# Masks of a sparse attention added by TensorE instead of VectorE, with a new order of the pieces (l2 attention of a twelve-stage decoder)

## The reference

```
ss = einsum('bhsd,bhmd->bhsm', q4, ks4) * SCALE
causal_sel = arange(s)[None, :, None] >= pos[:, None, :]
a_sel = _masked_softmax(ss, (causal_sel & valid[:, None, :])[:, None])
...
wmask = (cols <= rows) & (cols > rows - WIN)
a_win = _masked_softmax(sw, wmask[None, None])
...
g = softmax(x @ Wg + bg, axis=-1)
out = g[..., 0:1] * out_comp + g[..., 1:2] * out_sel + g[..., 2:3] * out_win
return out @ Wo + bo
```

## Time and profile before

| what | value |
|---|---|
| median of three runs | 2348.35 us (2347.89 to 2351.34) |
| the profiled execution, its own time | 2353.02 us |
| its span in the profile | 2351.2 us |
| TensorE busy | 1899.7 us, 81% |
| VectorE busy | 1656.8 us, 70% |
| ScalarE busy | 1021.0 us, 43% |
| GpSimd busy | 605.2 us, 26% |
| granted TensorE clock, mean | 0.843 |

### The profile page before, as it was taken

The page is one execution under the profiler, slowest core; times in us unless marked ns, Lnnn a source line. Parts: engine busy times, 40 slices in busy tenths (PEclk is TensorE's granted clock), DMA queues, the critical chain, the costliest instruction groups (busy, mean ns, idle before and its releaser), DMA issues. The chain is left out here.

```text
span 2351.2 us, 31000 instructions
## 1 busy us (share of the span) xinstructions
PE 1899.7 (81%) x11181; PEld 1074.3 (46%) x11186; DVE 1656.8 (70%) x3766; ACT 1021.0 (43%) x1648; POOL 605.2 (26%) x528
## 2 busy tenths in 40 slices
PE   4788888889788989999997677668885766699983
PEld 2444554536363333577775555545332322334321
DVE  6665848665678878644457988984479988976546
ACT  1226646464743635633332232232354446335562
POOL 0002324242331010000002633520146534631100
PEclk8888999989997777999998778766877877789955
DMA  4001213030402000000000000000000000000000
GB/s 168 1 0 47 58 31 74 10 95 1 103 2 93 1 1 1 23 1 1 1 1 10 1 1 1 1 1 1 0 1 0 0 0 0 0 1 1 1 5 14
DMA packets 19224, 44.32 MB, mean 19 GB/s; under 512 B 5323, under 2 KB 7935, under 8 KB 18047
## 3 DMA queue, kind: packets, MB, share of 16 engines
q1 hardware_dynamic: 19071, 42.33, 6.4%
HBM read 17.15 MB, written 1.05 MB: 8 GB/s over the span
## 5 line engine op out<-in xcount | busy, mean ns | idle before, releaser
L2440 POOL TENSOR_TENSOR l_attn_lane_u<-l_attn_lane_xp,l_attn_lane_bn 128x512 f32<-128x512 f32 x128 | 177.2, 1412 | 192.4 <-ACT l_attn_lane_bn L2411 152.3
L2358 PE MATMUL lane_banks<-l_attn_lane_hc,base 128*128 128x512 f32 x256 | 165.7, 764 | 58.3 <-DVE l_attn_lane_hc L2498 58.2
L2489 DVE TENSOR_TENSOR_SCAN l_attn_lane_h<-l_attn_lane_da,l_attn_lane_u 128x512 f32<-128x512 f32 x128 | 188.5, 1508 | 11.3 <-ACT l_attn_lane_da L2419 8.0
L604 POOL TENSOR_SCALAR lane_next_rstd<-lane_next_mv 128x4 f32<-128x4 f32 x48 | 12.2, 253 | 697.3 <-DVE lane_next_mv L581 697.2
L1728 ACT ACTIVATE l_ffn_lane_hT<-lane_banks,weights 128x512 f32<-128x512 f32 x128 | 87.9, 687 | 145.1 <-PE lane_banks L1682 144.5
L1774 DVE SCALAR_TENSOR_TENSOR l_ffn_lane_eo<-lane_banks,l_ffn_lane_sel,l_ffn_lane_eo 128x128 f32<-128x128 f32 x224 | 63.0, 344 | 101.4 <-PE lane_banks L1704 100.8
L1704 PEld LDWEIGHTS lane_banks<-weights,l_ffn_lane_hT 128*128 128x128 f32 x1024 | 119.8, 192 | 15.9 <-issue 12.2
L1526 ACT ACTIVATE l_attn_lane_ex<-lane_banks 128x512 f32<-128x512 f32 x160 | 84.1, 667 | 98.3 <-PE lane_banks L1440 97.6
L1704 PE MATMUL lane_banks<-weights,l_ffn_lane_hT 128*128 128x128 f32 x1024 | 122.8, 276 | 0.9 <-DVE l_ffn_lane_eo L1774 0.9
L2358 PEld LDWEIGHTS lane_banks<-l_attn_lane_hc,base 128*128 128x128 f32 x256 | 56.6, 238 | 131.9 <-DVE l_attn_lane_hc L2498 87.8
L2037 POOL TENSOR_TENSOR l_attn_lane_qb<-l_attn_lane_qT,base 128x512 f32<-128x512 f32 x64 | 87.8, 1382 | 97.8 <-PE lane_banks L1939 84.3
(11 more groups left out here) (525 smaller groups left out, 4685.5 us busy)
## 6 DMA issues: line engine op xcount, KB each, us to landing
f_attn_lane_vb<-f_attn_lane_work SPq DMA_DIRECT2D x192, 64.0 KB, 2.0
weights<-packed SPq DMA_DIRECT2D x1, 4564.5 KB, 13.4
f_attn_lane_work<-f_attn_lane_work SPq DMA_DIRECT2D x64, 64.0 KB, 2.0
f_attn_lane_vb<-f_attn_lane_va SPq DMA_DIRECT2D x8, 512.0 KB, 4.5
f_attn_lane_vb<-f_attn_lane_va SPq DMA_DIRECT2D x8, 384.0 KB, 5.9
weights<-packed SPq DMA_DIRECT2D x1, 2320.0 KB, 8.6
weights<-packed SPq DMA_DIRECT2D x1, 2091.0 KB, 14.1
weights<-packed SPq DMA_DIRECT2D x1, 1263.0 KB, 5.4
```

The costliest lines, as they stand in the source:

```text
L2358: pe.matmul(ps(2 + c), w("ident"), hc[:, c, :], start=(n == 1), stop=(n == NS)).then_inc(*s.up("state_added"))
L2440: g.tensor_tensor(u[:, i % 3, :], dtx[:, c, :], bn[:, n % 2, :], ALU.mult).then_inc(*s.up("u_ready"))
L2489: v.tensor_tensor_scan(h[:, c, :], da[:, i % 3, :], u[:, i % 3, :], 0.0, ALU.mult, ALU.add).then_inc(*s.up("scanned"))
```

## The change

In `l2_attn`:
- `mask` becomes 16-bit. TensorE puts it into the score bank first, as the 16-bit identity by the mask broadcast to four head groups, and the four score matmuls accumulate on top. `mask_ready` is new and is awaited before the first scores.
- ScalarE copies the finished scores from PSUM to `sc` and signals `masked`; VectorE's addition is gone.
- Tiles are scored eight ahead of the turns instead of five, so two groups are scored before the first is turned. VectorE's order becomes shift 0, shift 1, weigh 0, weigh 1, shift 2, pick 0, weigh 2, shift 3, pick 1, weigh 3, pick 2, pick 3. ScalarE takes the exps of groups 0 and 1 together after tile 7.
- GpSimd spreads ten tiles, multiplies groups 0 and 1, spreads the other six, and multiplies groups 2 and 3.
- The bias is added to x by GpSimd at the unit's start. The values of blocks and selected tokens are copied into `vall` by ScalarE after tile 2.

```diff
-    mask = sb("mask", [P, J, C])
+    mask = sb("mask", [P, J, C], BF16)
...
+        pe.wait_ge(*s.at("mask_ready", 1))
 
         def scores(j):
+
             yield
             if j >= 2:
                 pe.wait_ge(*s.at("masked", j - 1))
             pe.wait_ge(*s.at("qb_ready", j + 1))
+            bank = ps(j % 2)[:, 0:4 * C].rearrange("p (g c) -> p g c", g=4)
+            pe.matmul(bank, net.w16("ident16"), bc(mask[:, j, :], 4), start=True, stop=False)
             for g in range(4):
-                last = pe.matmul(ps(j % 2)[:, g * C:(g + 1) * C], qb[:, j % 2, tile(g)], kall[:, j, :], start=True, stop=True)
+                last = pe.matmul(bank[:, g, :], qb[:, j % 2, tile(g)], kall[:, j, :], start=False, stop=(g == 3))
             last.then_inc(*s.up("scores_in_psum"))
...
-        for i in range(J + 6):
-            if 5 <= i < J + 5:
-                yield from turn(i - 5)
+
+        for i in range(J + 2 * GR + 1):
+            if 2 * GR <= i < J + 2 * GR:
+                yield from turn(i - 2 * GR)
             if i < J:
                 yield from scores(i)
-            if i >= 6:
-                yield from values(i - 6)
+            if i >= 2 * GR + 1:
+                yield from values(i - 2 * GR - 1)
...
-            if i % GR == GR - 1 and i < J:
+            if i < J:
                 g = i // GR
+                yield
+                act.wait_ge(*s.at("scores_in_psum", i + 1))
+                if g >= 2:
+                    act.wait_ge(*s.at("pT_in_psum", i - 2 * GR + 1))
+                act.activation(sc[:, g % 2, i % GR, :, :], ps(i % 2)[:, 0:4 * C].rearrange("p (g c) -> p g c", g=4), ACT.Copy)\
+                   .then_inc(*s.up("masked"))
+            if i == 2:
+
+                yield
+                act.wait_ge(*s.at("cv_ready", 1))
+                act.wait_ge(*s.at("values_ready", 1))
+                act.activation(vall[64:C, :, :], bc(vcs[64:C, :], J), ACT.Copy).then_inc(*s.up("vall_ready"))
+            for g in {2 * GR - 1: (0, 1), J - 3: (2,), J - 1: (3,)}.get(i, ()):
                 yield
                 act.wait_ge(*s.at("shifted", g + 1))
                 act.activation(sc[:, g % 2, :, :, :], sc[:, g % 2, :, :, :], ACT.Exp, scale=scale).then_inc(*s.up("exp_ready"))
...
         yield
+        norm.wait(g_)
+        g_.tensor_tensor(x, x, bc(w("a2_bo"), NT), ALU.add).then_inc(*s.up("bias_added"))
+        yield
         g_.wait_ge(*s.at("q_ready", 1))
...
+        for i in range(2 * GR + 2):
+            yield from spread(i)
+        yield from weights(0)
+        yield from weights(1)
+        for i in range(2 * GR + 2, J):
+            yield from spread(i)
+        yield from norm.gpsimd(g_)
+        yield from weights(2)
+        yield from weights(3)
...
-        v.tensor_copy(vall[64:C, :, :], bc(vcs[64:C, :], J)).then_inc(*s.up("vall_ready"))
...
-                v.tensor_tensor(sc[:, g % 2, i % GR, :, :], ps(i % 2)[:, 0:4 * C].rearrange("p (g c) -> p g c", g=4),
-                                bc(mask[:, i, :], 4), ALU.add).then_inc(*s.up("masked"))
...
-        st.link(v.tensor_tensor(x, x, bc(w("a2_bo"), NT), ALU.add))
+        yield from shift(0)
+        yield from shift(1)
+        yield from weigh(0)
+        yield from weigh(1)
+        yield from shift(2)
+        yield from pick(0)
+        yield from norm.means(v, norm.to_come)
+        yield from weigh(2)
+        yield from shift(3)
+        yield from pick(1)
+        yield from weigh(3)
+        yield from norm.apply(v, norm.to_come)
+        yield from pick(2)
+        yield from pick(3)
         yield
         v.wait_ge(*s.at("y_in_psum", 1))
+        v.wait_ge(*s.at("bias_added", 1))
```

More of the change, by code:

```diff
@@ L2012, in scalar @@
                .then_inc(*s.up("vwin_ready"))
-        for i in range(J + 5):
-            if i >= 5:
-                j = i - 5
+        for i in range(J + 2 * GR):
+            if i >= 2 * GR:
+                j = i - 2 * GR
                 yield
@@ L2040, in gpsimd, with weights @@
         yield
+        norm.wait(g_)
+        g_.tensor_tensor(x, x, bc(w("a2_bo"), NT), ALU.add).then_inc(*s.up("bias_added"))
+        yield
         g_.wait_ge(*s.at("q_ready", 1))
-        yield from spread(0)
-        for i in range(J + 1):
-            if i + 1 < J:
-                yield from spread(i + 1)
-            if i >= GR and i % GR == 0:
-                g = i // GR - 1
-                if i == J:
-                    yield from norm.gpsimd(g_)
-                yield
-                g_.wait_ge(*s.at("weights_ready", g + 1))
-                g_.tensor_tensor(sevenths(g), sevenths(g), bci(wt7[:, g % 2, :, :].rearrange("p r n -> p (r n)"), 16), ALU.mult)\
-                  .then_inc(*s.up("probs_ready"))
+        def weights(g):
+            yield
+            g_.wait_ge(*s.at("weights_ready", g + 1))
+            g_.tensor_tensor(sevenths(g), sevenths(g), bci(wt7[:, g % 2, :, :].rearrange("p r n -> p (r n)"), 16), ALU.mult)\
+              .then_inc(*s.up("probs_ready"))
+        for i in range(2 * GR + 2):
[7 more added lines that the diff above has]
+        yield from weights(3)
     def vector(v):
@@ L2094, in vector @@
         v.wait_ge(*s.at("gates_ready", 1))
+        v.wait_ge(*s.at("seen_ready", 1))
         st.link(v.tensor_reduce(gm[:, :], gl[:, :, :], AX.X, ALU.max))
         v.tensor_tensor(gl[:, :, :], gl[:, :, :], bci(gm[:, :], 3), ALU.subtract).then_inc(*s.up("gates_shifted"))
-        st.step(v.tensor_scalar(msel, msel, NEG, None, ALU.mult))
+        v.tensor_scalar(msel, msel, NEG, None, ALU.mult).then_inc(*s.up("mask_ready"))
         yield
@@ L2102, in vector @@
         st.link(v.tensor_tensor(gl[:, :, :], gl[:, :, :], bci(gm[:, :], 3), ALU.mult))
-        yield
-        v.wait_ge(*s.at("values_ready", 1))
-        v.tensor_copy(vall[64:C, :, :], bc(vcs[64:C, :], J)).then_inc(*s.up("vall_ready"))
-        yield
-        v.wait_ge(*s.at("seen_ready", 1))
         def shift(g):
@@ L2154, in pick @@
                             r[:, g % 2, :, :].rearrange("p j (h q) -> p j q h", h=4), AX.X, ALU.add).then_inc(*s.up("o_ready"))
-        for i in range(J + 6):
-            if i < J:
-                g = i // GR
-                yield
-                v.wait_ge(*s.at("scores_in_psum", i + 1))
-                if g >= 2 and i % GR == 0:
-                    v.wait_ge(*s.at("pT_in_psum", GR * (g - 1)))
-                v.tensor_tensor(sc[:, g % 2, i % GR, :, :], ps(i % 2)[:, 0:4 * C].rearrange("p (g c) -> p g c", g=4),
-                                bc(mask[:, i, :], 4), ALU.add).then_inc(*s.up("masked"))
-                if i % GR == GR - 1:
-                    yield from shift(g)
-            if i == J:
-                yield from norm.means(v, norm.to_come)
-            if i % GR == 0 and GR <= i <= J:
-                yield from weigh(i // GR - 1)
-            if i == J:
-                yield from norm.apply(v, norm.to_come)
-            if i >= 9 and i % GR == 1:
-                yield from pick(i // GR - 2)
-        st.link(v.tensor_tensor(x, x, bc(w("a2_bo"), NT), ALU.add))
+        yield from shift(0)
[12 more added lines that the diff above has]
+        yield from pick(3)
         yield
         v.wait_ge(*s.at("y_in_psum", 1))
+        v.wait_ge(*s.at("bias_added", 1))
         ln.finish(v.tensor_tensor(x, x, by_tile(ps(0)), ALU.add))
```

## The result

The changed kernel takes 2322.41 us (median of 4 runs, 2319.51 to 2323.05) where the kernel before took 2349.85 (4 runs, 2347.89 to 2352.71): a ratio of 0.9878 with a 95% interval of 0.9866 to 0.9890, 27.4 us less. The forecast was 2307, with a range of 2283 to 2338.

The account below looks back on a forecast made before the run. VectorE was taken to bound the l2_attn stage of 340 us: 297.4 - 52.6 = 244.8 us at 82% gives 298.5, a gain of 41.5 us. With other stages at nothing the median was forecast at 2307 us, range 2283 to 2338.

Parts of the forecast that it names:

- my own case: l2_attn stage: VectorE's share 79 to 86%, stage 285 to 310 us, whole kernel 2293 to 2319 us; chance 0.57.
- the second rival: TensorE becomes the bound in the turning phases, at most 80% busy: stage 325 us, 15 us gained, 2333; chance 0.15.
- I keep the rest as it is.: l2_attn stage: removing 52.6 us of VectorE's work removes no stretch from the rest, leaving 244.8 of 297.4 us.
- Wrong: Signs against the forecast, among them VectorE's total busy time not lower by some 50 us, GpSimd's stretch replacing the additions.
- The share of 82%: l2_attn stage: VectorE busy 82%, between 87.5% now and 75%, so 244.8 / 0.82 = 298.5 us.
- The chain: l2_attn: a unit that never waits for the other lane shrinks from 133 to 106 us; floor by chains 233 us.
- Bias at nothing: l2_attn: four bias additions on GpSimd, 5.5 us, cost nothing; by the skill's rule, gain some 5 us less.
- TensorE 0.4 us, ScalarE 0.55 us each: l2_attn: signs for the 64 mask products and 64 score copies; at most 26.4 us on TensorE, 38 on ScalarE.
- Stages before and after at nothing, 8 us either way: Behind the l2_attn stage: same work, lanes nearer together, change costed at nothing, with 8 us to either side for the range.
- First: VectorE stays 87.5 to 90% full: stage 272 to 280 us, 60 to 68 us gained, 2280 to 2288; chance 0.17.
- Third, ScalarE's queue: Score copies stand behind exps that wait for shifts: up to 42 us slower, 2390, mostly 2352 to 2370; chance 0.09.
- The clock was to be above 0.76: l2_attn stage: sign that TensorE's granted clock rises above 0.76, from 0.73 in the steady piece before.

Follow-up runs that it names:

- all_but_order: The changed kernel with the order of the kernel before (lead of five tiles, groups one by one), planned anew: 2366.43 us, ratio 1.0054 to 1.0087 to the kernel before.

## Why the prediction was right, and where it was off

The direction and the mechanism held: VectorE bounds most of the stage, and relieving it with a shorter chain gains time. The size came out smaller, 27.4 us of the 41.4 that were forecast. The measured 2322.4 us lie outside my own case (2293 to 2319) and in the part of the range that I had opened for the second rival, which is not what happened. So that the range held is in part luck. Point by point:

- **"I keep the rest as it is."** This step failed. 297.4 - 52.6 = 244.8 us was to remain; in the stretch that answers it was 260.6, which is 15.8 more, since more of VectorE's small instructions were held by GpSimd's. The text named the symptom under "Wrong", VectorE's total not lower by some 50 us, and it came (19.5), but the sum priced it at nothing. With 260.6 in place of 244.8 the same formula gives 260.6 / 0.82 = 317.8 us, and 315.2 were measured, where 298.5 had been forecast.
- **The share of 82%** was right: 82.7% in that stretch. Its reason held too, for a part of the stage. VectorE's waits for score copies at a unit's third group (25.9 us, the longest 10.2) and behind them for values (10.6) add up to 36.5 us. In the long ones TensorE works without a gap, and they grew when its mask products were doubled.
- **The chain:** 106 instead of 133 us for a unit alone was never measured by itself, and the sum for it leaves out the exp (1.7 us) between shift and weights. Its role isn't settled. With the old order and the mask alone the stage became 7 us shorter, with the old order and all the rest 17.5 us longer. What is shown is that the whole gain needs both parts.
- **Bias at nothing:** right. The Trainium skill (SBUF — State Buffer, Who interferes with whom) would have made the gain 5 us smaller by these four additions; the stage is 337.1 with them on GpSimd and 337.2 without. The same rule, applied to the products, is what the sum lacked: it says that GpSimd's reads exclude VectorE's instructions with two SBUF inputs, and its writes don't. The gates' subtraction agrees (3253 ns at most beside a product, 209 beside a write). The clamps have one SBUF input and were held too; the page allows that for such instructions in a two-port mode. The scaling of the mask, one input as well, was held by a write, which fits that; no run here shows the mode itself.
- **TensorE 0.4 us, ScalarE 0.55 us each:** 353 and 544 ns. ScalarE has 136.7 us in the stretch for which 143 was said.
- **Stages before and after at nothing, 8 us either way:** the profiled executions differ by 4.0 us ahead of the stage and 4.8 behind it, with the same work. No run shows a cause for either in the edit, so 8.8 us of the profiled gain of 33.9 had no term in the forecast. The stretch itself gained 24.8 us of 41.5.
- **The rivals.** First: the share didn't stay at 87.5%. Second: TensorE is busy for 69% of the stretch, not 80, and sets the pace in the waits named above only. Third, ScalarE's queue: its exps wait 48.8 us for shifts now, longest 8.7 (29.4 and 5.2), but in VectorE's longest wait no exp stands ahead of the copies, and the change is faster. all_but_order was slower than before, but not that way: its exps wait 30.1 us, the longest 3.8.

The clock was to be above 0.76 and was 0.80.

## What to carry to other kernels

When work is taken from the fullest engine, look at what the rest of it will stand beside. Here the holds by GpSimd belonged to the place: making VectorE's instruction there shorter didn't help, and making GpSimd's shorter did. Here relief and order only paid together: mask and order brought 9.9 and 0 us alone and 27 together with the two small moves. Compare instructions of one kind before and after, since the sum over a stage can hide that some were held more and others less. And compare variants by the stage that was edited, since the same work behind it took 744 to 759 us.

## What the runs showed of the hardware

- An instruction of 48 columns on VectorE, 188 ns at its fastest, was held for 7.84 us while eleven spreads of GpSimd ran one after another. So a hold can outlast one GpSimd instruction. With the product in quarters, four instructions in 3.66 us one after another, the gates' subtraction was held for no more than the first of them (953 ns). What decides between the two wasn't tried.
- A GpSimd instruction that only writes 1792 columns (1609 ns) left the gates' subtraction, two inputs in SBUF, at 207 to 209 ns. It held the scaling of the mask, one input in SBUF and 219 ns at its fastest, for up to 1469 ns.
- 64 matmuls without use made the end of the program 8.6 us earlier, with the stage 2.9 us longer: from 32 to 44 us behind the stage the granted clock was 1.00, where it was 0.50 in the changed kernel. Whether those matmuls brought it there or chance did stays open, since executions of one kernel lay 15 us apart.
